# Second layer by head pairs: two heads' scores in row halves, values as the stationary operand in column halves

## What is computed

```python
def _L1_attn_ref(x, Wq, Wkv_down, Wk_up, Wv_up, Wo):      # 8 heads of 64
    q = (x @ Wq.T).reshape(b, t, 8, 64)
    kv_latent = x @ Wkv_down.T                             # width 64
    k = (kv_latent @ Wk_up.T).reshape(b, t, 8, 64)
    v = (kv_latent @ Wv_up.T).reshape(b, t, 8, 64)
    attn = softmax(einsum('bqhd,bkhd->bhqk', q, k) * scale)
    return einsum('bhqk,bkhd->bqhd', attn, v).reshape(b, t, 512) @ Wo.T

def _L1_ffn_ref(x, Wq, Wk, Ws, Wd, Wv, Wo):                # 8 heads of 64, 5 experts, 2 chosen
    wv = topk_mask(x @ Ws, 2) * sigmoid(x @ Ws)            # per head and expert
    v = einsum('bthe,btek->bhtk', wv, einsum('btd,edk->btek', x, Wv))
    attn = einsum('bhij,bhjd->bihd', softmax(q * scale @ k.T), v)   # q = x @ Wq, k = x @ Wk
    return einsum('bthe,bthk,ekd->btd', topk_mask(x @ Wd, 2), attn, Wo)
```

## Time and profile before

| | |
|---|---|
| Median of 3 runs | 4350.37 us (4325.01 to 4354.36) |
| The profiled execution | 4306.31 us, span 4304.6 us |
| PE busy | 3588.2 us, 83% |
| DVE, ACT, POOL busy | 2031.9, 1662.1, 1830.3 us |
| Granted PE clock, mean of the span | 0.757 |
| Second layer, 2020 to 4305 us | PE busy 2152.76 of 2285 us, clock 0.81 |

### The profile page before, as it was taken

The page is one execution under the profiler, slowest core; times in us unless marked ns, Lnnn a source line. Parts: engine busy times, 40 slices in busy tenths (PEclk is TensorE's granted clock), DMA queues, the critical chain, the costliest instruction groups (busy, mean ns, idle before and its releaser), DMA issues.

```text
span 4304.6 us, 40868 instructions
## 1 busy us (share of the span) xinstructions
PE 3588.2 (83%) x13001; PEld 1914.3 (44%) x13001; DVE 2031.9 (47%) x3645; ACT 1662.1 (39%) x2289; POOL 1830.3 (43%) x1518
## 2 busy tenths in 40 slices
PE   5777877777777845774989999999999999999898
PEld 2223333333223222331546565555655556565555
DVE  4788777787877721221223343333334334344322
ACT  1677666766667820110212222222223232233211
POOL 1444555565555754552002525334253442534352
PEclk7676667666676767886557888888889898899865
DMA  0000000000000015773000000000000000000000
GB/s 29 10 1 12 15 12 16 12 11 12 12 15 2 16 22 134 178 176 83 0 5 10 6 1 20 1 1 20 1 20 2 1 20 1 15 1 15 1 10 5
DMA packets 91847, 99.53 MB, mean 23 GB/s; under 512 B 19665, under 2 KB 87377, under 8 KB 91601
## 3 DMA queue, kind: packets, MB, share of 16 engines
q1 hardware_dynamic: 71120, 77.60, 6.0%
q0 software_dynamic: 20480, 19.03, 2.8%
HBM read 69.91 MB, written 22.48 MB: 21 GB/s over the span
## 4 chain that ended last, share of the span: by engine, by line
PE 40%; issue 9%; DVE 2%; POOLq 1%; POOL 1%; DVEq 0%; ACT 0%; DMA 0%; SPq 0%; ACTq 0%
PE S L1367 12%; PE OP L1386 11%; PE TP L1374 5%; PE BA L1287 4%; PE BD L1299 2%; PE BD L1356 1%; PE BD L1287 1%; POOLq L1640 1%; POOL GT L1649 1%; PE BD L1276 1%; PE BD L1328 1%; PE BD L1319 1%; PE BD L1338 0%; PE BA L1299 0%; POOL XN L1620 0%
## 5 line engine op out<-in xcount | busy, mean ns | idle before, releaser
L1445 ACT ACTIVATE PR<-S,NM 128x512 f32<-128x512 f32 x512 | 351.4, 686 | 1247.6 <-DVE NM L1562 1187.3
L1386 PEld LDWEIGHTS OP<-VN,PT 128*128 128x128 f32 x4096 | 605.0, 227 | 475.2 <-issue 459.2
L846 POOL TENSOR_TENSOR TT<-TT,SS 128x2048 f32<-128x2048 f32 x128 | 580.2, 4546 | 534.3 <-ACT SS L777 533.9
L1367 PE MATMUL S<-KT,QT 64*128 64x512 f32 x1024 | 701.7, 772 | 2.1 <-DVE VN L1478 1.6
L1386 PE MATMUL OP<-VN,PT 128*128 128x64 f32 x4096 | 680.6, 319 | 0.0
L370 PE MATMUL OB<-TT,VAL 128*17 128x512 f32 x1024 | 396.5, 885 | 76.1 <-ACT TT L785 75.9
L1562 DVE TENSOR_REDUCE NM<-S 128x1 f32<-128x512 f32 x512 | 349.8, 685 | 229.7 <-PE S L1367 223.3
L1374 PE MATMUL TP<-ident,PR 128*128 128x128 f32 x2048 | 375.3, 314 | 25.2 <-ACT PR L1445 22.8
L611 DVE TENSOR_SCALAR TT<-SC 128x1024 f32<-128x1024 f32 x256 | 311.6, 1217 | 138.6 <-PE SC L349 78.6
L1649 POOL TENSOR_TENSOR GT<-AH,MO 128x320 f32<-128x320 f32 x224 | 154.7, 722 | 487.1 <-DVE AH L1574 487.1
L1374 PEld LDWEIGHTS TP<-ident,PR 128*128 128x128 f32 x2048 | 291.5, 172 | 124.0 <-issue 89.1
(11 more groups left out here) (232 smaller groups left out, 4606.1 us busy)
## 6 DMA issues: line engine op xcount, KB each, us to landing
WG<-w_gu SPq DMA_DIRECT2D x64, 384.0 KB, 3.4
WD<-w_dn SPq DMA_DIRECT2D x64, 128.0 KB, 3.3
XL<-x SPq DMA_DIRECT2D x8, 512.0 KB, 4.1
X<-x SPq DMA_DIRECT2D x8, 512.0 KB, 4.0
rows<-XL SPq DMA_DIRECT2D x8, 512.0 KB, 9.1
slot_tokens<-TID,IDX POOLq DMA_INDIRECT x256, 6.7
stream<-X SPq DMA_DIRECT2D x8, 512.0 KB, 3.6
WD<-w_dn SPq DMA_DIRECT2D x64, 64.0 KB, 3.5
```

The costliest lines, as they stand in the source:

```text
L846: pool.tensor_tensor(tt, tt, ss, ALU.add).then_inc(sems["w"], 1)
L1367: pe.matmul(S[u % 2][:], QT[kind][r:r + DH1, h // 2, j * P:(j + 1) * P], KT[kind][r:r + DH1, h // 2, :], start=True, stop=True).then_inc(s ...
L1386: ins = pe.matmul(OP[h % 2][:, j, 0:DH1], PT[u % 2][:, m, :], VN[kind][:, m, h * DH1:(h + 1) * DH1], start=(m == 0), stop=(m == NT - 1))
L1445: act.activation(PR[u % 2][:], S[u % 2][:], ACT.Exp, bias=NM[:, u % 2:u % 2 + 1], accum_out=SM[:, h % 2, j:j + 1]).then_inc(sems["prob"], 1)
```

## The change

The second layer's loop is by head pairs. A step is a pair of heads and one query tile, 16 steps a run, and 16 runs (`RUNS`) are written out one after the other with no hardware loop.

- **Scores.** Two products, the first head on array rows 0 to 63 and the second on rows 64 to 127, into the two banks of `S[s % 2]`. There are four score banks for two steps. One DVE maximum covers both heads; ACT makes two exponentials.
- **Turn.** Eight transposes per step, into two banks; DVE copies the first head's, ACT the second's, into a `PT` that holds all four query tiles of the pair, twice.
- **Values.** The values of a head (64 columns) are the stationary operand and 512 columns of transposed probabilities move. The first head fills PSUM partitions 0 to 63 of `OT`, the second 64 to 127. One key tile is done in each step for the pair before, so the output of a pair comes out transposed, in one bank.
- **Shares.** In kind 1 DVE takes the reciprocals spread over 512 elements (`RB`), PE turns them by a product with the identity (`spread`), ACT copies that, and DVE multiplies `OT` into `AT1`: the transposes of the output go. In kind 2 ACT copies `OT` to `OS2`, PE transposes it back (`heads2`), and DVE scales it.
- **Items.** One bank `BK` in place of `BD` and `BA`; `READER` says who reads each. An item waits only for the last content of `BK` to be read. The tables are new and name a slot in the step: 1 between `turn` and `scores`, 2 and later behind `attend`. The prepare of batch 1 and the first and last runs carry items too. `X` is a ring of four batches, loaded ahead; the three buffers and their copies go.

```diff
+RUNS = [(1, 0), (1, 1)] + [r for b in range(B - 2) for r in ((2, b), (1, b + 2))] + [(2, B - 2), (2, B - 1)]
...
+OUT_1 = table((0, 0, 1, "product_out1", 0), (0, 1, 1, "product_out1", 1), (0, 1, 2, "product_out1", 2),
+              (0, 2, 1, "product_out1", 3), (0, 2, 3, "stats", 1))
...
+HEADS_1 = table((0, 7, 1, "spread", 0), (0, 11, 1, "spread", 1), (0, 15, 1, "spread", 2), (1, 3, 1, "spread", 3),
+                (0, 7, 2, "heads1", 0), (0, 11, 2, "heads1", 1), (0, 15, 2, "heads1", 2), (1, 3, 2, "heads1", 3))
...
-    S = [ps(f"S{i}", [P, N]) for i in range(2)]
+    S = [ps(f"S{i}", [P, 2, N]) for i in range(2)]
     TP = [ps(f"TP{i}", [P, N]) for i in range(2)]
-    OP = [ps(f"OP{i}", [P, NT, P]) for i in range(2)]
-    BD, BA = ps("BD", [P, N]), ps("BA", [P, N])
+    OT = ps("OT", [P, N])
+    BK = ps("BK", [P, N])
...
+    READER = dict(
+        turn_norm="dd", latent="a", queries1="aaaa", keys1="dada", values1="adad", product_out1="dddd", gates="d",
+        experts="aaaa", queries2="aaaa", keys2="aaaa", turn_out2="ddd", product_out2="dddd",
+    )
...
-            def operands_in(v):
-                if v.all_due("free_d"):
-                    pe.wait_ge(sems["free_d"], v.value)
-                if v.all_due("free_a"):
-                    pe.wait_ge(sems["free_a"], v.value)
...
+            def item(v, release):
+                if v.holder and v.all_due(v.holder):
+                    pe.wait_ge(sems[v.holder], v.value)
+                v.holder = release
+                v.tally(release).add(1)
+                return BK
...
-            def scores(v, kind, u):
-                h, j = u // NT, u % NT
-                r = DH1 * (h % 2)
-                if u == 0:
-                    operands_in(v)
-                pe.matmul(S[u % 2][:], QT[kind][r:r + DH1, h // 2, j * P:(j + 1) * P], KT[kind][r:r + DH1, h // 2, :],
-                          start=True, stop=True).then_inc(sems["s"], 1)
...
+            def spread(v, pair, b):
+                bank = item(v, "spread_in")
+                pe.wait_ge(sems["rs"], v.next("rs"))
+                for j in range(NT):
+                    ins = pe.matmul(bank[:, j * P:(j + 1) * P],
+                                    RB[:, 2 * j:2 * j + 2, :].rearrange("p h d -> p (h d)"), ident[:], start=True, stop=True)
+                ins.then_inc(sems["item_a"], 1)
...
+            def heads2(v, pair, b):
+                bank = item(v, "head")
+                if v.all_due("ot"):
+                    pe.wait_ge(sems["ot"], v.value)
+                for j in range(NT):
+                    ins = pe.transpose(bank[:, j * P:(j + 1) * P], OS2[:, j * P:(j + 1) * P], ident[:])
+                ins.then_inc(sems["item_d"], 1)
...
+            def scores(v, r, s):
+                kind, b = RUNS[r]
+                pair, j = s // NT, s % NT
                 if j == 0:
-                    if v.due("head", 2):
-                        pe.wait_ge(sems["head"], v.value)
+                    need(v, f"queries{kind}", b, pair)
+                    need(v, f"keys{kind}", b, pair)
+                for h2 in range(2):
+                    lo = DH1 * h2
+                    ins = pe.matmul(S[s % 2][:, h2, :], QT[r % 2][lo:lo + DH1, pair, j * P:(j + 1) * P],
+                                    KT[r % 2][lo:lo + DH1, pair, :], start=True, stop=True)
+                ins.then_inc(sems["s"], 1)
+            def turn(v, r, s):
+                for h2, way in enumerate("da"):
+                    if v.due("in_" + way, 1):
+                        pe.wait_ge(sems["in_" + way], v.value)
+                    pe.wait_ge(sems["prob"], v.next("prob"))
+                    for m in range(NT):
+                        ins = pe.transpose(TP[h2][:, m * P:(m + 1) * P], PR[s % 2][h2][:, m * P:(m + 1) * P], ident[:])
+                    ins.then_inc(sems["turned_" + way], 1)
+            def attend(v, r, pair, m):
...
+                if m == 0:
+                    if v.all_due("ot"):
+                        pe.wait_ge(sems["ot"], v.value)
+                    for way in "da":
+                        if v.all_due("in_" + way):
+                            pe.wait_ge(sems["in_" + way], v.value)
...
-                for m in range(NT):
-                    ins = pe.matmul(OP[h % 2][:, j, 0:DH1], PT[u % 2][:, m, :], VN[kind][:, m, h * DH1:(h + 1) * DH1],
...
+                for h2 in range(2):
+                    h, lo = 2 * pair + h2, DH1 * h2
+                    ins = pe.matmul(OT[lo:lo + DH1, :], VN[r % 2][:, m, h * DH1:(h + 1) * DH1], PT[pair % 2][h2][:, m, :],
                                     start=(m == 0), stop=(m == NT - 1))
-                ins.then_inc(sems["pv_" + "da"[u % 2]], 1)
...
+                if m == NT - 1:
+                    ins.then_inc(sems["pv_out"], 1)
...
+            for r, s in steps():
+                if r < TAIL:
+                    turn(v, r, s)
+                carry(v, parts, r, s, 1)
+                if ahead(r, s):
+                    scores(v, *ahead(r, s))
+                rr, pair = behind(r, s)
+                if rr >= 0 and rr < TAIL and (r < TAIL or s < NT):
+                    attend(v, rr, pair, s % NT)
+                carry(v, parts, r, s, 2, 3, 4)
...
+                for h2 in range(2):
+                    act.activation(PR[s % 2][h2][:], S[s % 2][:, h2, :], ACT.Exp, bias=NM[:, s % 2, h2:h2 + 1],
+                                   accum_out=SM[:, pair % 2, j, h2:h2 + 1]).then_inc(sems["prob"], 1)
...
+            def set_down(v, pair, b):
+                act.wait_ge(sems["pv_out"], v.next("pv_out"))
+                act.activation(OS2[:], OT[:], ACT.Copy).then_inc(sems["ot"], 1)
...
+                dve.tensor_reduce(NM[:, s % 2, :], S[s % 2][:], AX, ALU.max, negate=True).then_inc(sems["peak"], 1)
...
+            def shares(v, r, pair):
+                dve.wait_ge(sems["prob"], v.next("prob", 2 * NT))
+                if RUNS[r][0] == 1:
+                    dve.reciprocal(RB[:], SM[:, pair % 2].rearrange("p j h -> p (j h)").unsqueeze(2)
+                                   .to_broadcast([P, 2 * NT, DH1])).then_inc(sems["rs"], 1)
+                else:
+                    dve.reciprocal(RS[:, pair % 2], SM[:, pair % 2]).then_inc(sems["rs"], 1)
+            def heads1(v, pair, b):
+                dve.wait_ge(sems["spread_in"], v.next("spread_in"))
+                dve.wait_ge(sems["pv_out"], v.next("pv_out"))
+                dve.tensor_tensor(AT1[:, pair, :], OT[:], RBT[:], ALU.mult).then_inc(sems["ot"], 1)
```

663 lines of the change are left out of this document (325 added, 338 removed), and 3 rows, old and new, of the table PREP_1.

## The result

The changed kernel takes 3488.93 us, the median of 4 runs (3480.0 to 3501.69), against 4337.69 us for the kernel before in the same comparison. The ratio is 0.804, with a 95% interval of 0.8011 to 0.8069: 850 us less. Forecast were 3680 us and a range of 3540 to 3930. The sign was right; the size was too small by 190 us.

The account below looks back on a forecast made before the run. TensorE was taken as the bound: 1744 - 507 + 34 = 1271 us of work, at clock 0.90 1412, plus 209 idle, 1621 us instead of 2285; the execution of 3642 times 1.010 gave 3680 us, range 3540 to 3930.

Parts of the forecast that it names:

- The step's length: TensorE time of one new step: transposes 0.98, packed scores 1.05, packed values 1.05, together 3.08 us against 5.06 for two units.
- The work: TensorE work in the second layer at the full level: 1744 - 507 + 34 = 1271 us.
- The clock: TensorE's granted clock in the second layer: 0.90, from 0.88 in the middle with projections between units; ends 0.81 and 0.95.
- The idle time: TensorE idle in the second layer: 132 + 39 + 38 = 209 us.
- The reciprocal's 39: First attention: DVE's 512-element reciprocal, 32 times, delays the copy TensorE waits for by 1.2 us each, 39 us.
- The value products, put at 38: First value product of each pair waits for copies of the transposes just issued, about 0.6 us x 64 = 38 us.
- the 132 taken over from before: TensorE's 132 us of idle time in the old second layer, kept; single projection bank and DVE's selection work were put in it.
- The factor of 1.010: Median of the runs shown over the profiled execution: turns 3642 us into the forecast 3680 us.
- Clock at 0.95: Rival: second-layer clock 0.95 instead of 0.90, giving 3604 us; 66% for 3604 to 3837, the forecast included.
- partial packing: Rival: a packed pair of score or value products costs 0.18 us more than 0.86, giving 3782 us; 5%.
- The slower case: Rival: the clock stays at the half level, so 1271 us of work becomes 2542 and the time 4820 us; 3%.
- Better than the range: Rival: no new idle time and a clock near 1, a time below the forecast range; 2%.

Follow-up runs that it names:

- the alternating kernel: Changed kernel with both old product forms, each step doing transposes, scores and values of one head, then of the other: 3901.47 us, 0.8967 of the kernel before.
- the statistics split: Kernel before with only the layer norm statistics on DVE made a token tile at a time instead of in one block: 4145.02 us, 0.9537.
- the kernel with both old forms: Changed kernel with thin value products (probabilities stationary, 64 value columns moving) and both heads' scores on one row half: 3846.22 us, 0.8846 of the kernel before.
- the kernel with the small reciprocal: Changed kernel with DVE taking 8 reciprocals and copying them to 512 elements, instead of 512 reciprocals: 3463.16 us, 0.7961 of the kernel before.

## Why the forecast was right about the products and too high in its number

**The step's length: right.** 3.08 us forecast, 3.09 measured. Row halves and column halves both run side by side in f32: the scores' block is 0.86 us shorter than in one half and the values' block 0.81 shorter than at full width, where one full product is 0.86. The Trainium skill ("TensorE: Matmul & The Clock Gate", Measured speedup vs the span model) has 2.38x for three column tiles of 32 columns, which makes 0.79 per tile. Two tiles of 64 columns here turn 1.72 us of products into 0.91, 0.94 per tile, and two row halves into 0.86, 1.0 per tile; the measurement decides. The Trainium skill says too that changing the tiling mode drains the engine ("TensorEngine Tiling (Array Packing)", Key Properties). The runs price only borders between blocks: three more in a step, two of them with a change of mode, cost 77 us of work over 256 steps, 0.3 us a step, and how much of it is the mode no run separates.

**The work: right.** 1271 us forecast, 1270 measured. Of the 1744 us before, the forms took 1680 - 1270 = 410 and blocks of two heads in place of one 77, and some 13 came back, since the alternating kernel, which makes the spread too, has 1757.

**The clock: the step that failed.** I took 0.90 over PE's busy time, from the mixed middle's 0.88, "since nearly all steps are now mixed". It is 0.957 (and 0.94 as the mean of the stage). The same work of 1270 us so takes 1327 us and not 1412: 85 us, the largest part of the miss. What I did not ask was why the middle had 0.88. I took it as what this mixture of instructions is granted. It was the mean of the full level and of 14 stretches at the half level, 13 of them behind a pause that the change happened to remove; the trace had them, and I read no row on either side of one. With the statistics split the old units have 0.96 in the middle. The value lies just above my upper bound of 0.95.

**The idle time: too high by 56 us.** 209 forecast, 153 measured. The reciprocal's 39 were fair (26 us by experiment, clock included). The value products, put at 38, wait 2.6 us in all; in the rows above the scores stand between the copied transposes and them. And of the 132 taken over from before, the pauses behind the statistics and most of those of the prepare went, while POOL is waited for in two places where I had put nothing: 34.5 us in the middle for its normalisation and 44.8 near the end for its gating, where the kernel before has 17.7 and 6.6 in all. I had costed POOL by its mean load of some 800 us in 1600; the waits come from where it stands in a chain.

**The factor of 1.010: 50 us, and chance.** The profiled execution was forecast at 3642 and took 3501.69; that is 140 us, which the clock and the idle time make up (85 and 56). The other 50 us between 3680 and 3488.93 are the factor: the kernel before had been profiled in an execution below its median, the changed kernel was profiled in its slowest.

**The rivals.** "Clock at 0.95" came nearest, at 3604; partial packing, only one form packed and no packing are ruled out by the blocks. The slower case, a half clock all through, has no support: the new forms come up within 13.7 us with nothing to help. "Better than the range", at 2%, was where it fell. It wanted "no new idle and a clock near 1"; the clock was near 1, and new idle time there was (POOL's), though less than what went.

**Where the 850 us are.** 357 are the forms of the products (3846 to 3489), 55 the blocks of two heads (3901 to 3846), and some 440 the rest: the timetable, the pauses, the two runs that stood alone, the program written out without a loop and the ring of inputs. The shares go by this order of undoing; another order could give others. Of those 440 the statistics' place in the kernel before explains about 195 by itself (158 between the two profiled executions: about 15 us of idle time and 149 for the half level). Of the remaining 245, the first and last runs are the likely larger part: their stretches of 187.7 and 189.6 us became 64.9 and 61.5 in the alternating kernel, and half of that difference is 125 us. That part was not tried alone, and the other 120 are not accounted for one by one. So the larger half of the gain comes from what the title of the change doesn't name.

## What to carry to other kernels

A mean granted clock is not a property of a mixture of instructions. Before using it as a price, list the stretches at the half level and read what stands on both sides of each: the pause before and the first block at the full level behind. A block of 2 us on VectorE in front of a short, regular chain cost ten times its own pause here; split it into pieces that fit into the slack of one unit, or put dense projections right behind it. Where the half level covers time in which PE stands idle, as in the tail here, weigh the clock by PE's busy time, or the work comes out too small. And when a rewrite changes both the form of the work and its schedule, undo the form alone: here it was less than half of the gain.

## What the hardware showed that I had not expected

- The time to come back from the half level depends on what is run: mostly 3.4 to 6.8 us in the changed kernel, 13.7 us at the start of new steps alone, 54.6 us in old forms by blocks of two heads and 109.2 us when they alternate (both up to a spread), and 13.7 to 44.4 us behind the pauses in the kernel before. In that kernel's first run the half level stayed for 147.5 us in which PE was never idle.
- A pause of 1.65 to 1.82 us lost the level 13 times in the kernel before, and yet one of 1.22 us in every empty step (scores one step ahead) left the clock at 0.95. In the kernel with both old forms nine of 13 pauses of 1.88 or 2.01 us lost it and four did not.
- A slower form of one product gave back time elsewhere: 189 us of work became 126 us of time.
- A DVE reciprocal is priced by its elements, 178 ns for 4, 1145 for 160 and 3343 for 512, some 6.2 ns each, while a copy of 512 takes 685 ns. In the kernel with the small reciprocal, 8 reciprocals and the copy that spreads them took 193 and 947 ns.
